# A decoder block on one core: the values' product moves to the end of each attention step, and VectorE's late adds are reordered

## What is computed

```python
x = x + attn(layernorm(x))                     # 16 heads of 64, causal penalty of -50
x = x + xattn(layernorm(x), ctx)               # 16 heads of 64, no mask
x = x + ffn(layernorm(x))

# attention, for each head
scores = q @ k.T / 8                           # + penalty
out = softmax(scores) @ v                      # then out @ Wr, summed over heads

# ffn
shared = swiglu(flat @ w_in.T) @ w_out.T
h = swiglu(flat @ w1.T)                        # 512 wide
routed = sum(h * weight[:, e] @ w2[e].T for e in chosen 2 of 8)
```

## Time and profile before

| | |
|---|---|
| time, median of 3 runs | 853.43 us (852.5 to 854.44) |
| the profiled execution | 858.67 us, span 856.9 us |
| mean granted clock of PE | 0.972 |
| PE busy | 794.4 us, 93% of the span |
| DVE, ACT, POOL busy | 424.0, 448.2, 284.6 us |
| attention | from the start to about 599 us |
| experts (39 tiles) | about 710 to 789 us |
| from the first gather to the end | 791.5 to 856.9 us |

### The profile page before, as it was taken

One profiled execution on the slowest core, in us unless ns is written; L12 is line 12 of the kernel. 1 busy time (PEld: TensorE's weight loads), 2 busy tenths in 40 slices (PEclk: granted clock), 3 DMA queues, 4 the chain that ended last, 5 costly groups with the idle time before them and its releaser, 6 DMA issues. The chain is left out here.

```text
span 856.9 us, 16919 instructions
## 1 busy us (share of the span) xinstructions
PE 794.4 (93%) x5859; PEld 665.0 (78%) x5859; DVE 424.0 (49%) x1263; ACT 448.2 (52%) x1475; POOL 284.6 (33%) x310
## 2 busy tenths in 40 slices
PE   7999999999999999999999999999999768999931
PEld 6788888888888877888888888888777658998731
DVE  4565465365455735434543543555767442332253
ACT  4765555565565756566565565566445224553210
POOL 1543125115123634532351262162102660000554
PEclk9999999999999999999999999999999987999966
DMA  7795000000000111000000002000501446773233
GB/s 226 274 416 155 2 0 0 0 0 0 0 0 26 51 33 42 2 25 1 0 24 0 0 0 98 1 25 2 197 1 49 172 171 195 213 207 108 74 112 110
DMA packets 33607, 64.53 MB, mean 75 GB/s; under 512 B 3412, under 2 KB 15060, under 8 KB 32980
## 3 DMA queue, kind: packets, MB, share of 16 engines
q1 hardware_dynamic: 29460, 51.27, 18.2%
q0 software_dynamic: 4096, 12.59, 4.4%
HBM read 38.02 MB, written 30.02 MB: 79 GB/s over the span
## 5 line engine op out<-in xcount | busy, mean ns | idle before, releaser
L411 POOL TENSOR_TENSOR prob<-prob,rsum 128x512 f32<-128x512 f32 x128 | 132.8, 1040 | 345.4 <-DVE rsum L591 345.4
L484 ACT ACTIVATE prob<-psS,nmin 128x128 f32<-128x128 f32 x512 | 182.4, 386 | 11.7 <-DVE nmin L575 6.6
L484 ACT ACTIVATION_READ_ACCUMULATOR prob<-psS,nmin 128x1 f32 x512 | 116.0, 227 | 0.0
L575 DVE CUSTOM_DVE_ANT_0 psS<-psS,mask 128x128 f32<-128x128 f32 x256 | 65.2, 329 | 66.5 <-PE psS L709 66.5
L464 ACT ACTIVATE v<-psW 128x512 f32<-128x512 f32 x64 | 38.2, 597 | 110.2 <-PE psW L144 110.2
L468 ACT ACTIVATE pT<-psT 128x512 f32<-128x512 f32 x64 | 38.2, 597 | 80.8 <-PE psT L721 79.9
L142 PE MATMUL psA<-wo_lo,oT_hi 128*128 128x256 f32 x256 | 78.8, 308 | 0.0
L578 DVE TENSOR_REDUCE nmin<-psS 128x4 f32<-128x512 f32 x64 | 41.2, 685 | 71.8 <-PE psS L709 71.8
L709 PEld LDWEIGHTS psS<-kt,q 64*128 64x128 f32 x1024 | 62.1, 187 | 17.9 <-issue 15.7
L732 PEld LDWEIGHTS psT<-pT,v 128*64 128x64 f32 x1024 | 54.7, 136 | 26.7 <-issue 26.7
L709 PE MATMUL psS<-kt,q 64*128 64x128 f32 x1024 | 74.4, 285 | 0.0
(11 more groups left out here) (249 smaller groups left out, 1921.2 us busy)
## 6 DMA issues: line engine op xcount, KB each, us to landing
hs<-zero SPq DMA_DIRECT2D x1, 9984.0 KB, 30.5
stage<-hs SPq DMA_DIRECT2D x39, 256.0 KB, 2.9
ys<-z SPq DMA_DIRECT2D x39, 128.0 KB, 1.9
w_lo<-w_raw SPq DMA_DIRECT2D x4, 1024.0 KB, 8.2
stage<-ctxT SPq DMA_DIRECT2D x4, 512.0 KB, 4.2
out<-xres SPq DMA_DIRECT2D x16, 128.0 KB
xres<-x SPq DMA_DIRECT2D x3, 512.0 KB, 7.8
stage<-wq SPq DMA_DIRECT2D x2, 512.0 KB, 5.0
```

The lines of the kernel that those rows point to most:

```text
L411: nc.gpsimd.tensor_tensor(prob[:, r, :], prob[:, r, :], rsum[:, r].unsqueeze(2).broadcast_to([P, TPG, P]), ALU.mult).then_inc(prob_done, 1)
L484: e = nc.scalar.activation(prob[:, n, :], flat(psS[:])[:, n * P:(n + 1) * P], ACT.Exp, bias=nmin[:, n:n + 1], scale=-1.0, accum_out=psums[ ...
L575: m = nc.vector.tensor_tensor_reduce(sc, sc, mask[:], 1.0, LARGE, ALU.add, ALU.min, nmin[:, i * TPG + n:i * TPG + n + 1])
```

## The change

In the attention phase PE's step ends with `weighted_values`; the second head's transposes go between the q product and the k product; `v_project` goes from steps 0 to 3 to steps 1 to 4. ACT and DVE accordingly split the output of step s at the start of step s + 1. In the feed-forward part PE does unit H9 ahead of `shared_out(1)`, DVE does `add_shared(0)` ahead of the splits of group 1 and `add_shared(1)` behind unit H9; in the end, DVE's `add_routed` and `add_shared` stand between the last units. The work is the same.

```diff
@@ ACT, in step @@
+                    if depth > 1:
+                        oT_split(s - 1, j % 2)
-                    if not first:
+                    if depth > 0:
                         pT_copy(s)
...
-                    if not first:
-                        oT_split(s, (j + 1) % 2)
-                    if j < TPG:
-                        v_copy(G, 1, j, 0)
+                    if 1 <= j <= TPG:
+                        v_copy(G, 1, j - 1, 0)
...
                 act.preload_act_table(ACT.Silu)
+                oT_split(STEPS - 1, 0)
                 pT_copy(STEPS)
@@ PE @@
-                def qk_project(sub, G, j):
+                def qk_project(sub, G, j, between=lambda: None):
...
                     for n, (hi, lo) in enumerate(sources):
+                        if n == K:
+                            between()
...
+                def p_transposes(s, i, first=False):
+
+                    pe.wait_ge(prob_done, 2 * s + i - 1)
+                    if not first and i == 1:
+                        pe.wait_ge(oT_lo, s - 1)
+                    for n in range(TPG):
+                        mm = nc.tensor.transpose(psT[:, i, n * P:(n + 1) * P], prob[:, i * TPG + n, :], ident[:])
+                    mm.then_inc(pT_mm, 1)
...
+                    def second_half():
+                        if depth > 0:
+                            p_transposes(s, 1, first=depth == 1)
+
                     scores(s, first=depth == 0)
                     if depth > 0:
-                        p_transposes(s, first=depth == 1)
+                        p_transposes(s, 0)
                     if j + 1 < PAIRS:
-                        qk_project(sub, G, j + 1)
+                        qk_project(sub, G, j + 1, second_half)
...
-                        weighted_values(s, (j - 1) % PAIRS)
...
                         out_project((j - 2) % PAIRS, j % 2)
-                    if j < TPG:
+                    if 1 <= j <= TPG:
...
                     if j == PAIRS - 1 and after < 2:
                         v_first_half(after, G + 1)
+                    if depth > 0:
...
+                        weighted_values(s, (j - 1) % PAIRS)
@@ DVE, feed-forward part @@
+                add_shared(0)
                 for m in range(HT):
                     u = UNITS.index(f"S1{m}") + 1
                     if u > 14:
                         unit(u)
                     split(f"S1{m}")
-                    w2_lo_part(m)
-                add_shared(0)
+                    if m < HT - 1:
+                        w2_lo_part(m)
+                unit(UNITS.index("H9"))
+                w2_lo_part(3)
                 add_shared(1)
                 split("S20")
...
                 dve.wait_ge(weights_known, 2)
-                for T in range(B):
-                    if T == 2 * TPG:
-                        add_shared(2)
+                unit(UNITS.index("S21"))
+                for T, name in enumerate(("S22", "S23", "S30")):
+                    u = UNITS.index(name)
+                    unit(u)
+                    split(UNITS[u - 1])
+                    add_routed(T)
+                add_routed(3)
+                add_shared(2)
+                for T, name in enumerate(("S31", "S32", "S33"), TPG):
+                    u = UNITS.index(name)
+                    unit(u)
+                    split(UNITS[u - 1])
+                    add_routed(T)
+                split("S33")
+                for T in range(2 * TPG - 1, B):
+                    if T == 3 * TPG:
                         add_shared(3)
                     add_routed(T)
@@ PE, feed-forward part @@
                 unit("S20")
+                unit("H9")
                 shared_out(1)
-                for T in range(9, B):
+                for T in range(10, B):
                     unit(f"H{T}")
```

More of the change, by code:

```diff
@@ L521, in _ @@
                         first_hi(3)
-                step(0, 0, 0, first=True)
-                for j in range(1, PEEL):
-                    step(0, j, 0)
+                for j in range(PEEL):
+                    step(0, j, 0, depth=j)
                 with act.Fori(0, NGRP - 1) as G:
@@ L712, in scores @@
                                 mm.then_inc(s_mm, 1)
-                def p_transposes(s, first=False):
-                    for i in range(2):
-                        pe.wait_ge(prob_done, 2 * s + i - 1)
-                        if not first and i == 1:
-                            pe.wait_ge(oT_lo, s - 1)
-                        for n in range(TPG):
-                            mm = nc.tensor.transpose(psT[:, i, n * P:(n + 1) * P], prob[:, i * TPG + n, :], ident[:])
-                        mm.then_inc(pT_mm, 1)
+                def p_transposes(s, i, first=False):
[5 more added lines that the diff above has]
+                    mm.then_inc(pT_mm, 1)
                 def weighted_values(s, j):
@@ L787, in _ @@
                 v_first_half(0, 0)
-                step(0, 0, 0, 0, depth=0)
-                for j in range(1, PEEL):
-                    step(0, 0, j, 0, depth=min(j, 2))
+                for j in range(PEEL):
+                    step(0, 0, j, 0, depth=j)
                 with pe.Fori(0, NGRP - 1) as G:
@@ L806, in _ @@
                     step(1, 2 * NGRP - 1, j, 2)
-                p_transposes(STEPS)
+                p_transposes(STEPS, 0)
+                p_transposes(STEPS, 1)
                 out_project(PAIRS - 2, 0)
```

46 lines of the change are left out of this document (22 added, 24 removed).

## The result

| | before | after |
|---|---|---|
| time, median | 852.96 us (4 runs, 851.33 to 854.44) | 828.50 us (4 runs, 827.79 to 829.82) |
| the profiled execution | 858.67 us | 828.65 us, span 826.8 |
| mean granted clock of PE | 0.972 | 0.982 |

The ratio is 0.9715 (95% interval 0.9693 to 0.9738): 24.5 us less, where I had forecast 35.8. The time lies inside the range of 809 to 830 and 10.9 us above the predicted 817.6.

The account below looks back on a forecast made before the run. It took TensorE (PE), busy 93% of the span, as the bound, with GpSimd's indirect DMAs and VectorE's adds setting the end: -12.8 - 5.5 - 17.5 = -35.8 us from the 853.4 us median gave 817.6, range 809 to 830.

Parts of the forecast that it names:

- Usual step, -12.0 + 1.0 us in 63 steps: PE's attention steps: fewer width changes save 0.19 us each, 12.0 in all; transposes between q and k cost 1 us.
- values to scores: PE's change from half-width values to half-width scores in a step: taken as 0.20 us, bounds 0.11 and 0.32.
- Rivals 1 and 2: Attention: width changes cost more, +7.6 + 5.3 us at most (0.15); no cost between the two half-width modes, -5.7 us (0.10).
- Stalls, -4.3 us: Attention: three PE waits of 3.4 us go, plus 1.7 us of lowered clock, 0.8 given back: net 4.3 us less.
- Ends, +2.5 us: Attention's ends: 1.0 us more as step 0's v product moves, 1.5 us more by the Silu table load.
- oT_lo hidden: Attention: output's low part ready about 1.5 us after the last values, second transposes due at 3.1: cover 1.6 us.
- Rivals 4 and 5: Slower, oT_lo late in every step, 854 us or more (0.03); nothing gained, savings waited for elsewhere, 853 us (0.01).
- Scatters, -5.5 us: Feed-forward: with H9 earlier GpSimd's scatters run without a stop at 1.365 us each, the last at 699.2, not 704.7.
- Last part, -17.5 us: Adds between the last units: gathers run without a stop at 1.32 us, the end comes 17.5 us earlier.
- Rival 3: Last part: gathers run slower beside adds, some 3 us, or 15 us if each waits out one add; chance 0.08.
- "I subtract from the median": The 35.8 us sum, read from a profiled execution of 858.7 us, was taken off the median of 853.4.
- my own case: Whole kernel: the predicted terms hold and the time lies within 812 to 823 us; chance 0.62.

Follow-up runs that it names:

- the two single feed-forward parts: Kernel before with only H9 and the first add moved, 851.96 us (0.9978); kernel before with only the adds set between the last units, 841.93 us (0.9848).
- The attention part alone: Kernel before with the changed attention part and the feed-forward part as it was: 842.38 us, ratio 0.9867.
- the second profile: Kernel before, unchanged, run and profiled once more: 856.24 us in one run, span 854.5.
- all four kernels: Changed kernel with w2 splits halved, 839.57 us; first v product in step 0, 836.05; Silu table load behind the copy, 835.15; these together, w2 splits last, 841.18.
- the kernel with everything together: Changed kernel with first v product in step 0, Silu load behind the copy, w2 splits behind the last unit and halved: 841.18 us beside 859.02 (0.9793).
- the kernel with the splits in halves: Changed kernel with each of VectorE's eight w2 splits cut in two instructions at the same place: 839.57 us beside 859.02 (0.9771).
- The other two kernels of that chip: Changed kernel with the first group's first v product in step 0, 836.05 us (0.9731); changed kernel with Silu load behind the copy, 835.15 us (0.9730).

## Why the prediction was right in direction and 10.9 us too low

- **Usual step, -12.0 + 1.0 us in 63 steps: right.** Step for step of its kind, the changed one is 0.181 us shorter on average, 11.4 us in all, against 11.0. The unknown price, values to scores, is 0.20 to 0.21 us, as taken. So going from column halves to row halves does cost what the other changes of width cost here. The Trainium skill, TensorEngine Tiling (Array Packing), section Tiling Modes (Key Properties), says that a change of tiling mode drains TensorE; the trace agrees, with 0.20 to 0.21 us where the pace is 0.11. Rivals 1 and 2 fell. That the nearest row gave just this price for a pair that no row showed was an assumption that came out, not something the rows had settled.
- **Stalls, -4.3 us: 3.5.** Step 28's 0.7 us went; step 33 lost 3.8 us before and 0.99 after (I had given back 0.8). In the profiles of the two single feed-forward parts, whose attention is as before, step 33 lost only 2.25 us; the granted clock stayed at 1.00 from 313 to 341 us there, where both profiles of before show 0.92 to 0.96, so against those the attention stretch gains 10.5 us, not 12.1. The loss that I put down to the clock is there in some executions only (two of four with the old attention part). The attention part alone gained 11.4 us by its time.
- **Ends, +2.5 us: 2.8,** 1.4 at each. But the one at the end was misread: the table is 0.4 us of it.
- **oT_lo hidden: right.** 1.65 us against 1.5, no wait in a usual step. Rivals 4 and 5 fell.
- **Scatters, -5.5 us: 2.3, or 1.9 by the time of this part alone.** "13 intervals ... are 1.365 us each", carried over to the new order, is the step that failed. The pace of scatters was not theirs: it depends on which of VectorE's two-input instructions they meet, and the change moved the splits of w2 onto them (2.5 us). Another 1 us was a late signal in the profile of before.
- **Last part, -17.5 us: 13.0 by the time of this part alone.** The new end was right to 0.1 us (44.8 behind the first gather, forecast 44 to 45; gathers at 1.354, forecast 1.32). The old one was wrong: 62.3 us was the profiled execution's, 57.7 to 59.4 are the kernel's. Rival 3 was right in kind: gathers beside adds took 1.05 us and not 1.00, 1.5 us in all (where the sum had 1.016 each), most of it as with the scatters, a tenth of what each gather waiting out one add would have cost. The 10.9 us that the sum takes from the start of the last shared product to its add come from the second product and have its late signal in them: here it is 7.5 (807.18 to 814.69), and the last add waits for its gather, not for PE's product.
- **"I subtract from the median": wrong.** Two signals came late in the profiled execution alone, both in stretches that the change shortens (3.6 us on the second shared product, 5.2 on the fourth); set against the second profile they made those stretches 1.1 and 4.6 us longer, about its 5.3 us above the median. A sum made against it must be subtracted from it, or the excess be found first; both rows were in front of me. With these corrections (2.3 of attention, 3.2 of scatters, 4.5 of the last part) the sum is 25.8 us, where 24.5 were measured. They are read from the runs after the fact, so that agreement tests nothing new.
- **The range held by luck.** 828.5 us lies outside the 812 to 823 that I gave my own case and where rival 1 had put it (823 to 830), but dearer width changes, rival 1's reason, did not come; the profile of one slow execution and the longer scatters did.

## What to carry to other kernels

When the profiled execution is slower than the median, find out where before subtracting anything: an excess inside the stretch that the change removes is counted as gain. Where GpSimd issues indirect DMAs on the critical path, look at what VectorE does 0.125 us after each begins: a split with two SBUF inputs added its whole rest (113 scatters), an instruction with an input in PSUM 14 ns at most; short adds did so in three cases of four. And a transpose that waits for a copy two engines away is worth moving behind other work even when the usual step shows no wait, since the rare late steps pay for it.

## Not expected: signals of PE that come late beside indirect DMAs

On the second chip, all four kernels show this at the third shared product: PE (three rows), POOL (two) and DVE (one) of the kernel with the first v product in step 0.

```profile
793.31 0.28 PE L144 MATMUL psA<-wout_hi,hid_lo 128*128 128x256 f32 x1
793.43 0.40 PE L142 MATMUL psT<-zlo,wq_hi 128*128 128x512 f32 x1
...
803.92 0.63 PE L144 MATMUL psS<-zhi,wq_lo 128*128 128x512 f32 x1
802.09 1.00 POOL L992 DMA_INDIRECT stage<-ys,slot  x1 [0.30 <-issue]
808.92 0.99 POOL L992 DMA_INDIRECT stage<-ys,slot  x1 [5.83 <-DVE xres L1356]
805.27 1.29 DVE L1324 TENSOR_TENSOR xres<-psA,xres 128x512 f32<-128x512 f32 x2 [15.34 <-remote]
```

The product's last matmul starts at 793.31, but its signal comes at 805.25, 11.66 us after the recorded end (`remote` says that the profile finds no instruction ending near the signal). Those of the next two units come 0.12 and 0.25 us behind it, though their matmuls are recorded over 10 us. All three were released 2.2 us after the end of the last gather (802.09 + 1.00), when the gathers had stopped for want of buffers. In the others the third product's signal is late by 11.66 to 11.70 us too, and the stretch from the first gather to the last add takes 53.0 to 53.4 us, not 44.8. The fourth product's is late by 1.05 to 1.35 us in all four, with no stop of the gathers.

Two of the four show it earlier as well, and they are the two with shorter scatters. In the kernel with everything together the second shared product was late by 8.25 us, with ten scatters at their undisturbed pace between its start and its signal. In the kernel with the splits in halves it was late by 1.0 us, and the units H10, H11 and H12 behind it by 2.5, 6.1 and 2.8 us; H11's last matmul, ScalarE's Silu that waited for it, and the stop of the scatters behind that:

```profile
670.71 0.40 PE L144 MATMUL psS<-w_hi,z_lo 128*128 128x512 f32 x1
677.23 0.60 ACT L1000 ACTIVATE silu<-psS 128x512 f32<-128x512 f32 x1 [4.86 <-remote]
679.32 1.27 POOL L976 DMA_INDIRECT hs<-stage,slot  x1 [3.18 <-DVE stage L1201]
```

There the shorter scatters' gain went. The other two kernels of that chip, whose scatters are those of the changed kernel, show 0.01 us at the second product and the units behind it. On the first chip no signal of a product or a unit is over 0.1 us late in any of the eight kernels, the one with the shortest excess included. The late signals in the first profile of before (3.6 and 5.2 us, and 0.6 at the third product; on which chip it ran is not known) look the same: the two long ones were released 2.3 us after the last scatter or gather ahead of a stop.

So on that chip later signals of PE went with faster scatters. That the one makes the other is not shown: it rests on two kernels with one profile each. What holds the signals back, why on one chip and not on the other, and whether the recording of the profile has a part in it stay open.
